# The place of the W loads in SyncE's queue: behind the load of phases instead of at the end of each step

## What is computed

```python
# layer 0
y = conv1d(x, L0_cond_weight, taps=9, pad=4, groups=4) + (cond @ c_weight.T)[:, :, None] + bias
y_q = round(y / (max|y| of its row / 127));  w_q = round(W0 / (max|W0| of its row / 127))
x = x + fp16((y_q @ w_q.T) * scales)
# layer 1
agg_w, agg_b = expert mixing of 8 matrices 64x64 by softmax(mlp(cond))
x2 = agg_w @ x + agg_b
H = x2 @ W + b                                  # W is L1_ffn_W, 1024 x 1024
z = x2 @ A;  weights from H[:, odd, :8] and z   # soft top-2 of 8 experts
x = x + H + ((z * p_mix) @ Bmat) * 0.5
```

## Time and profile before

| | |
|---|---|
| median of 3 runs | 614.74 us (613.66 to 615.96) |
| profiled execution | 616.81 us |
| its span, first to last instruction | 615.0 us |
| TensorE busy | 599.2 us, 97% |
| VectorE, GpSimd, ScalarE busy | 434.6, 374.8, 356.9 us |
| DMA | 136.24 MB, 222 GB/s over the span |

### The profile page before, as it was taken

One profiled execution on the slowest core, in us unless ns is written; L12 is line 12 of the kernel. 1 busy time (PEld: TensorE's weight loads), 2 busy tenths in 40 slices (PEclk: granted clock), 3 DMA queues, 4 the chain that ended last, 5 costly groups with the idle time before them and its releaser, 6 DMA issues.

```text
span 615.0 us, 16175 instructions
## 1 busy us (share of the span) xinstructions
PE 599.2 (97%) x6467; PEld 343.3 (56%) x6500; DVE 434.6 (71%) x883; ACT 356.9 (58%) x622; POOL 374.8 (61%) x252
## 2 busy tenths in 40 slices
PE   8999999989999999999999999999999999999998
PEld 4656766667767777676554444444444444444444
DVE  5978999978999999997788667654535454355543
ACT  3879998889999999976644343544243333321100
POOL 3326555447766666655797946889877659656200
PEclk8999999999999999999999999999999999999999
DMA  8979988778999898783074115855455346532111
GB/s 339 351 207 297 382 306 295 266 273 299 332 322 328 323 320 314 262 309 139 37 284 163 34 45 193 314 206 194 172 182 200 118 164 237 207 141 99 70 68 69
DMA packets 38632, 136.24 MB, mean 222 GB/s; under 512 B 5036, under 2 KB 5580, under 8 KB 38513
## 3 DMA queue, kind: packets, MB, share of 16 engines
q1 hardware_dynamic: 33518, 118.43, 54.7%
q10 hardware_dynamic: 5040, 16.78, 6.8%
HBM read 87.95 MB, written 47.24 MB: 220 GB/s over the span
## 4 chain that ended last, share of the span: by engine, by line
PE 86%; issue 2%; DVE 1%; ACT 0%; DVEq 0%
PE ps L909 41%; PE ps L612 15%; PE ps L517 9%; PE ps L709 7%; PE ps L596 4%; PE ps L891 2%; PE ps L581 2%; PE ps L657 2%; PE ps L652 1%; PE ps L621 1%; PE ps L625 0%; PE ps L692 0%; DVE yb L1459 0%; PE ps L677 0%; ACT zT L1097 0%
## 5 line engine op out<-in xcount | busy, mean ns | idle before, releaser
L612 PE MATMUL ps<-wqT,yq_both 128*128 128x512 bf16 x479 | 115.2, 378 | 5.6 <-issue 4.6
L1284 POOL TENSOR_TENSOR x<-x_in,f_all 128x512 f32<-128x512 f32 x64 | 74.3, 1161 | 49.4 <-DVE f_all L1496 49.2
L1288 POOL TENSOR_TENSOR x_split<-x_ph,x_split 128x1032 f16<-128x1032 f32 x25 | 53.7, 2148 | 55.5 <-ACT x_split L995 55.5
L1022 ACT ACTIVATE yv<-yb,yinv 128x128 f32<-128x128 f32 x256 | 77.8, 388 | 0.8 <-DVE yinv L1487 0.8
L1323 POOL TENSOR_TENSOR ring<-ring 128x512 f32<-128x512 f32 x56 | 72.7, 1299 | 4.3
L612 PEld LDWEIGHTS ps<-wqT,yq_both 128*128 128x128 bf16 x512 | 45.5, 99 | 46.0 <-issue 1.2
L1496 DVE SCALAR_TENSOR_TENSOR f_all<-ps,tok_scale,wsc_b 128x512 f16<-128x512 f32 x64 | 47.9, 749 | 18.8 <-PE ps L612 17.9
L517 PE MATMUL ps<-x_split,conv_h 128*64 128x256 f16 (+1 forms) x1248 | 60.1, 274 | 0.0
L517 PEld LDWEIGHTS ps<-x_split,conv_h 128*64 128x64 f16 (+1 forms) x1248 | 47.5, 108 | 9.8 <-issue 7.9
L1816 DVE SCALAR_TENSOR_TENSOR x_in<-ps,unscale,x_in 128x512 f32<-128x512 f32 x30 | 22.5, 750 | 39.9 <-PE ps L909 39.8
L1816 DVE SCALAR_TENSOR_TENSOR wst<-ps,unscale,wst 128x512 f32<-128x512 f32 x27 | 20.3, 750 | 36.7 <-PE ps L909 36.7
(11 more groups left out here) (351 smaller groups left out, 1322.2 us busy)
## 6 DMA issues: line engine op xcount, KB each, us to landing
x_in<-in_x SPq DMA_DIRECT2D x32, 512.0 KB, 6.1
x_scratch<-x SPq DMA_DIRECT2D x32, 512.0 KB, 3.6
x_ph<-in_x_phases SPq DMA_DIRECT2D x31, 516.0 KB, 5.1
x_scratch<-ring SPq DMA_DIRECT2D x26, 512.0 KB, 5.2
ring<-x_scratch SPq DMA_DIRECT2D x26, 512.0 KB, 5.4
x_in<-x_scratch SPq DMA_DIRECT2D x12, 512.0 KB, 3.8
out<-x_in ACTq DMA_DIRECT2D x12, 512.0 KB, 3.6
wst<-in_w_rows SPq DMA_DIRECT2D x10, 512.0 KB, 6.7
```

What stands on the lines that cost most here:

```text
L612: last = mm(acc_bank(t, h), yqT[:, t % 2, p, :], wqT[:, p, h * HALF:(h + 1) * HALF], start=p == 0, stop=p == PH - 1)
L1022: last = A(yv[:, s, :], yb[:, t % 2, s, :], ACT.Copy, scale=yinv[:, s:s + 1], bias=MAGIC)
L1284: g.tensor_tensor(x1[:, t % 2, s], x_in[:, t % 3, s], f16[:, s], ALU.add).then_inc(sem("x1_ready"), 1)
L1288: g.tensor_tensor(x_split[:, (t - SPLIT) % 2, 1, :], phases(t), x_split[:, (t - SPLIT) % 2, 0, :], ALU.subtract).then_inc(sem("xl_ready"), 1)
```

## The change

In each step of SP's loop, the three conditions that load pieces of W move from behind the load of x to right behind the load of phases. They keep their waits. Steps without a W load are not touched, and no other engine's code changes.

```diff
                 if c >= 3 and c + LEAD + 1 < NT:
                     load_phases(c + LEAD + 1)
+                if 0 <= c + 1 - W_ABS < NL:
+                    load_w(c + 1 - W_ABS)
+                if c + 2 in split_steps:
+                    load_w(NL + split_steps.index(c + 2))
+                if c + 1 in sum_steps:
+                    load_ws(sum_steps.index(c + 1))
                 if c >= 3:
                     save_x1(c - 3)
                 if c >= 4 and c - 4 < SAVED:
                     save_x2(c - 4)
                 if c == 2:
                     load_phases(4)
                 if 3 <= c < NT:
                     load_x(c)
-                if 0 <= c + 1 - W_ABS < NL:
-                    load_w(c + 1 - W_ABS)
-                if c + 2 in split_steps:
-                    load_w(NL + split_steps.index(c + 2))
-                if c + 1 in sum_steps:
-                    load_ws(sum_steps.index(c + 1))
```

## The result

The change took the kernel from 614.17 us (612.52 to 615.96, 6 runs) to **621.14 us** (618.96 to 622.85, 6 runs): a ratio of 1.0097, 95% interval 1.0076 to 1.0118. The forecast was 614.7 us with a range up to 617.5. It was wrong.

The account below looks back on a forecast made before the run. TensorE, busy 599.2 of 615.0 us, was taken as the bound. The 24 moved loads summed to 0 us on the path, so the forecast was the median itself, 614.7 us, range 612.5 to 617.5.

Parts of the forecast that it names:

- the even steps 12 to 26: SP's loop: two W loads leave at once behind phases, their waits already over; cost 0 in each of eight steps.
- The first part: What bounds the kernel: TensorE, busy 97%; no DMA wait in the loop, so only making an in-time transfer late costs time.
- Gaps in TensorE's issue: Rival: TensorE's three unexplained gaps at the mixing, 2.2 us, vanish or double, 612.5 to 616.9; 15% for over 1 us.
- Steps 3 to 5: SP's loop: W has no new wait, stores and x leave one issue, about 0.45 us, later; cost 0.
- phases come late: Rival: W right behind phases slows their landing, phases 7 first; 616.1 to 653 us; 8% for more than 0.5%.
- Steps 6 to 9: SP's loop: W newly waits for w_abs, 2.35 us in step 6; store of x1 0.7 to 1.4 us late; cost 0.
- Step 16 of SP's queue: Worked case: W goes at 150.0 behind phases at 149.62, 4.4 us earlier, its issues over before the store's turn.
- the list of what would show the prediction right: Signs: TensorE busy 599 us, same chain, four new W waits of some 10 us, no DMA wait in the loop.

Follow-up runs that it names:

- the two halves: The change with only the W loads of steps 2 to 9 moved, 616.16 us, and with only those of steps 12 to 26 moved, 621.19 us.
- the four steps between: The kernel before with only the eight W loads of steps 14, 18, 22 and 26 moved behind phases: 616.17 us, ratio 1.0009.
- The early loads moved alone: The kernel before with only the W loads of steps 2 to 9 moved behind phases: 616.16 us, ratio 1.0023.
- the change with 58 instructions added: The change plus 116 already met semaphore waits (58 instructions) ahead of TensorE's first convolution: 630.52 us, ratio 1.0235.
- the kernel with added copies: The kernel before plus two 512 KB copies within DRAM issued behind phases in steps 12, 16, 20 and 24: 626.43 us, ratio 1.0178.
- the kernel with sixteen loads moved: The change with the eight W loads of steps 12, 16, 20 and 24 back at their old place: 615.56 us, ratio 0.9996.

## Why the prediction was wrong

**The step that failed** is the one on the even steps 12 to 26. It said: "Nothing is pushed back. Their bytes, 2.5 us at 414 GB/s, pass ahead of the stores, whose users are steps away. ... Cost 0 in each of the eight steps." The size of the bytes and the users of the stores are right. What is false is "nothing is pushed back". A packet that SP does not issue, TensorE's next 256 instructions, is pushed back by them. In steps 16, 20 and 24 it waited 3.3 to 5.4 us instead of 1.5 to 2.1, and its slack is 2.3. Measured on the two halves, these loads cost 6.1 us of the 7.0, and the eight in steps 12, 16, 20 and 24 alone 5.3. In the four steps between, the predicted 0 is not contradicted (1.3 us between the medians; by the ratio 0.6, from -0.8 to 2.0).

**Why it was missed.** The first part said that the only way to cost time is to make a transfer late that is now in time. That was right, but I then looked only at transfers that the program issues and engines wait for by semaphore. The page lists another kind of traffic, q8 instruction, and I put no term on it.

**The rival "Gaps in TensorE's issue"** had the mechanism: gaps from full DMA engines, made or removed by another spacing of W. It failed in its size. I bounded it by "or make as many more", 2.2 us, without a reason that ties the number of gaps before to the number after. There were 4.4 us more, and the granted clock, which the rival didn't count at all, added about 1.7 in the profiled execution and fell in three of the six. Its sum should have been 614.7 + 4.4 = 619.1 for an execution without the fall and 620.8 with it; those groups took 619.8 and 622.2. Since the 4.4 is the difference of one pair of executions, it could not have come closer but by luck. I also used the Trainium skill's "mostly hidden" as one end and wrote that the 1.5 us gap speaks against it, and then did not follow the row. It was the row that was right.

**Steps 3 to 5 and "phases come late"**: cost 0 was right. Phases land sooner, 4.5 us in the median instead of 5.1, and ScalarE never waits for them. The longest landing in the loop is 7.4 us both before and after, so W behind them did not make them late. That rival is ruled out.

**Steps 6 to 9**: the new wait is what was worked out. In step 6 phases goes at 60.53 and W at 63.25, where 2.35 us of waiting behind phases' issue were predicted and 63.25 - 60.86 = 2.39 came. The four waits make 12.0 us, "some 10" predicted. Nobody waits for the store or for x. The early loads moved alone cost 1.1 us (0.4 to 2.5), which I had at 0; no experiment says what in them costs it.

**Step 16 of SP's queue** came as written: phases, and W 0.38 us behind.

```profile
147.83 0.33 SPq L315 DMA_DIRECT2D x_ph<-in_x_phases  x1
148.21 0.43 SPq L366 DMA_DIRECT2D wst<-in_w_rows  x1
148.69 0.43 SPq L376 DMA_DIRECT2D row_bias<-in_w_nat  x1
150.99 0.33 SPq L354 DMA_DIRECT2D x_scratch<-x  x1
```

So nearly every item of the list of what would show the prediction right came true, and the time was still outside the range. The list checked the transfers that I had thought of. It held nothing on the gaps, though they were the only idle time of the bounding engine in the loop.

The base was sound: the median of before is 614.17 over six runs, three of them those that the prediction had (614.74).

## What to carry to other kernels

Where the bounding engine stands in the middle of a row of equal instructions with nothing to wait for, look at the instruction queue in the DMA view: its 16 KB packets share the DMA engines with your data, and each has a deadline that the code ahead of the boundary sets. A burst issued just behind the boundary of a block that is executed fast is paid for beyond the slack of that block, and the same burst in the next step may be free; so a DMA issue that "nobody waits for" has a cost only the placement decides. Before costing a moved burst at zero, mark the block boundaries of the bounding engine and see which of them the burst comes in front of.

## What the runs showed of the hardware that was not expected

- A fetch can't use the time that is left of a block to the full: 1.3 to 1.5 us pass between the end of the packet (0.9 to 1.0 us itself in most cases, up to 2.7) and TensorE's next instruction.
- The packet waits while the DMA engines carry data, up to 8.0 us in the change with 58 instructions added, 7.5 in the kernel with added copies and 7.0 in the kernel before, there in a block that takes 9.3 us. The Trainium skill (DMA: Bandwidth & Descriptors, section on queues, rings and completion order) says that an engine round-robins between its queues at packet granularity, a whole packet of typically 9 to 17 and at most 64 descriptors at a time, so a packet on another queue would have its turn after one of these. In 5.2 us q1 moved 473 of the profile's packets, about 30 on each of the 16 engines, and q8 none. If one of these is a descriptor, that speaks against a turn after 9 to 17 of them, though not after 64, unless the request itself was late. No run shows which it is, so this stays open.
- The waits given here count from TensorE's own crossing. Behind the loop, in the final product (L909), the packets of the changed kernel start 0.8 to 4.3 us ahead of that crossing (341.3 against 345.6 us for the first), so there the fetch is asked for before TensorE has reached the boundary. When it is asked for in the mixing, the trace does not show.
- Single stops of TensorE were followed by 3.41 us at 1.2 GHz within 1.5 us. It was so behind each gap of 2.0 us or more in the loop (2.02, 2.15, 2.33, 2.47 and 2.88 us, in five kernels) and behind the 2.0 us that before waited in its start for the convolution's taps. Of five gaps from 1.75 to 1.92 us, two were followed by it (1.79 and 1.86) and three were not (1.75, 1.83 and 1.92).
- A wait that is already met is not free. In the start, 116 of them (58 instructions) ahead of the first convolution opened a gap of 6.06 us and 256 (128 instructions) one of 13.62 us, about 53 ns for each wait, with the clock at 1.2 GHz for part of it.
- Executions of one kernel differ in their gaps: step 13 has 1.48 us in the profile before, and none in that of the kernel with sixteen loads moved, whose program is the same around that step. The spread of 3 us between runs of a kernel is of that size. That it comes from there is likely, but was not tested.
